# Attention denominators of a three-stage transformer block: two split fp32r products instead of one plain fp32 product

## The chip, the cores and the metric

The kernel runs on one core of one Trainium2 chip. Its time is the device time of one execution in microseconds (us). The engines are named as in the profile: PE (TensorE matmul; PEld is its weight load), DVE (VectorE), ACT (ScalarE), POOL (GpSimd) and SP (SyncE, which here only issues transfers).

## The reference, cut to what matters

The block has three parts: cross attention, a causal linear attention with 16 heads of 64, and a mixture of 8 experts. The change lies in the second part:

```python
q = jax.nn.elu(q) + 1.0
k = jax.nn.elu(k) + 1.0
k_cum = jnp.cumsum(k, axis=1)
kv = jnp.cumsum(k[..., None, :] * v[..., :, None], axis=1)
numerator = jnp.einsum('bthj,bthij->bthi', q, kv)
denominator = jnp.einsum('bthj,bthj->bth', q, k_cum)
out = numerator / (denominator[..., None] + 1e-06)
```

The kernel computes this by masked scores: per batch entry and head it forms k times q (32 x 32), multiplies it by the causal mask (the tile `att`), and the denominator is the sum of `att` over the keys.

## The kernel before, in words

There are 64 batch entries of 32 tokens. Four entries make a tile of 128 rows, and there are 16 tiles. The cross attention goes tile by tile and lasts to about 130 us. The linear attention goes in 8 steps r of two tiles each, from about 132 us to 423 us, with a drain after the last; the experts fill the rest.

In the linear attention the large products are made of fp32 values split in two fp32r halves: `mm3` issues hi times hi, hi times lo and lo times hi (lines L437 to L439). Small products and the denominators are plain fp32.

Every engine runs its own program, written out in order, and the engines meet by semaphores only. In step r the order on each engine is this.

- PE (`astep` under `block.tensor`): eight blocks of q and k columns (`a_qks`, blocks 0 to 7, 12 matmuls each), with the denominators of step r-1 (`a_dens`, L611) between block 1 and block 2; then four blocks of gate columns (`a_gates`); then `a_nums` of step r-1 (L623) and `a_values`, once for each of the two tiles; the transposes for step r+1; then `a_proj` of step r-1 and `a_scores` (L602), again per tile. Block n of q and k from 4 on may start only when DVE has finished block n-4 of the same step (it takes over the PSUM bank), and gate block n only when DVE has finished block n+4. `a_nums` needs the normalised `att`.
- ACT: for every block Relu and Exp (L870, L873), with the copies of the denominators (`den_ev`, L897) between block 1 and block 2; then four Tanh for the gates, the high halves of the gated output (`gated_hi`, L892) and the copies of the values. From step 2 on a step ends in a Sqrt (L916) for the next layer norm, and then the next Exp has to load its function table first (ACT_TABLE_LOAD). So steps 3 to 7 begin with such a load, and steps 1 and 2 don't.
- DVE: `masks` (L1152) makes `att` of step r-1 out of the scores; `elu` (L1161) finishes each of the blocks 0 to 7 after its Exp; between them stand the four reciprocals of the denominators (`recip`, L1169) and the two multiplications by them (`norm_att`, L1174); then the layer norm rows, `gated` (L1181), `gated_lo` (L1191) and more.
- SP loads the weights of the experts (L348), 2 MB for each, into places that the attention's tiles leave free one after the other. Expert 1 is loaded right after the cross attention's last inputs, the other seven from the end of the linear attention on. The experts' first step waits for all eight.

Of the kernel before, what the change touches and what calls it, by code (L numbers as in the profile page):

```python
# [16 lines left out]
P = 128  # L17
# [57 lines left out]
def wait(eng, sem, value):  # L75

    if isinstance(value, int) and value <= 0:
        return
    eng.wait_ge(sem, value)
# [24 lines left out]
def build(nc, ctx, a, out):  # L104
# [10 lines left out]
    def place(name, shape, dtype=F32, where="low"):  # L115
        n = 4
        for d in shape[1:]:
            n *= d
        t = nc.alloc_sbuf_tensor_at(name, shape, dtype, offset=at[where])
        at[where] += (n + 31) // 32 * 32  # L120
        return t
# [67 lines left out]
    den = place("den", [P, 2, FC * 2 * T], where="late")  # L189
    neg = place("neg", [P, 2, 512], where="late")  # L190
    ex = place("ex", [P, 2, 512], where="late")
    w_out_lo = place("w_out_lo", [P, FC, D], F32R, "late")
    goh = place("goh", [P, FC, 2 * P], F32R, "late")
    assert at["late"] <= TOP_ADDR - 2 * DC * 4 * HF * 4
# [72 lines left out]
    def sem(name):  # L267
# [24 lines left out]

    (g_part, g_var, g_sq, g_rs, g_ln, g_tr, g_xT, g_mm, g_sc, g_max, g_idx, g_keep) = (sem("g_" + n) for n in (
        "part", "var", "sq", "rs", "ln", "tr", "xT", "mm", "sc", "max", "idx", "keep"))
    r_step, r_d, r_e1, r_both, r_rank, r_what, r_in, r_tab, r_map, r_done = (
        sem("r_" + n) for n in ("step", "d", "e1", "both", "rank", "what", "in", "tab", "map", "done"))
    o_init = sem("o_init")
# [13 lines left out]
    def _(sp):  # L311
# [35 lines left out]
        def load_expert(e):  # L347
            sp.dma_start(w13[:, e, :, :, :].rearrange("p w c h -> p (w c h)"), a["w13"][e, :, :]).then_inc(l_w13, 16)  # L348

        load_expert(1)  # L350
        sp.wait_ge(a_v, 4 * NT // 2)
        for e in range(E // 2, E):
            load_expert(e)
        sp.wait_ge(a_num, NT)
        sp.wait_ge(a_y, NT // 2)
        for e in (2, 3):
            load_expert(e)
# [76 lines left out]
    def _(pe):  # L434
# [171 lines left out]
                m.then_inc(a_sc, 1)  # L606

        def a_dens(r):
            wait(pe, a_att, 2 * r + 2)
            for s in range(2):  # L610
                pe.matmul(ps[:, 4 + s, :], con[:, C_TWOS:C_TWOS + P], att[:, s, :, :, :].rearrange("p c h t -> p (c h t)"),  # L611
                          start=True, stop=True).then_inc(a_den, 1)

        def a_nums(r, s):
            wait(pe, a_norm, 2 * r + s + 1)
# [23 lines left out]
        def astep(r, u):  # L639
            before = valid(r - 1, NR)  # L640
            wait(pe, a_lo, r + 1)
            a_qks(r, range(0, 2))
            if before:
                a_dens(r - 1)
            a_qks(r, range(2, 8))
            a_gates(r)
            for s in range(2):
                if before:
                    a_nums(r - 1, s)
                a_values(r, s)  # L650
            a_trs(r + 1)
            for s in range(2):
                if before:
                    a_proj(r - 1, 1 - u, s)
                a_scores(r, s)
# [133 lines left out]
    def _(act):  # L789
# [96 lines left out]
        def gated_hi(r, u, s):  # L886
# [3 lines left out]
            for k in range(2):  # L890
                cs = slice(4 * k, 4 * k + 4)
                act.activation(goh[:, cs, rows], goT[:, u, cs, rows], ACT.Copy).then_inc(a_gh, 1)  # L892

        def den_ev(r):
            for s in range(2):
                wait(act, a_den, 2 * r + s + 1)
                act.activation(den[:, s, :], ps[:, 4 + s, :], ACT.Identity, bias=con[:, C_EPS2:C_EPS2 + 1]).then_inc(a_de, 1)  # L897
# [24 lines left out]

        def astep(r, u):
            before = valid(r - 1, NR)
            elu_parts(r, range(0, 2))
            if before:
                den_ev(r - 1)
            elu_parts(r, range(2, 8))
            gates(r, u)
            for s in range(2):  # L930
                if before:
                    gated_hi(r - 1, 1 - u, s)
                values(r, s)
            a_hi_ev(r + 1)
            if r == 0:
                w_out_round()
            g_sqrt(r - 2)

        def drain(r, u):
            for k in range(3):  # L940
                g_xT_ev(k)
            den_ev(r)
            for k in range(3, 6):
                g_xT_ev(k)
            g_sqrt(r - 1)
            gated_hi(r, u, 0)
            g_xT_ev(6)
            gated_hi(r, u, 1)
            g_sqrt(r)
            g_xT_ev(7)  # L950

        a_hi_ev(0)
        for r in range(NR):
            astep(r, r % 2)
# [80 lines left out]
    def _(dve):  # L1035
# [112 lines left out]
        def masks(r):  # L1148
            mask = con[:, C_MASK:C_MASK + T].rearrange("p (a b t) -> p a b t", a=1, b=1).to_broadcast([P, 2, FC, T])
            wait(dve, a_sc, r + 1)  # L1150
            for h in range(2):
                dve.tensor_tensor(att[:, :, :, h, :], ps[:, 4 + h, :].rearrange("p (s c t) -> p s c t", s=2, c=FC), mask,  # L1152
                                  ALU.mult).then_inc(a_att, 1)

        def elu(r, n):
            if not valid(r, NR):
                return
            wait(dve, a_e, 8 * r + n + 1)
            wait(dve, a_sc, r)
            dst = kT if n % 2 else qT  # L1160
            dve.scalar_tensor_tensor(dst[:, n // 2 * 2:n // 2 * 2 + 2, :].rearrange("p c n -> p (c n)"), ps[:, n % 4, :], 0.0,  # L1161
                                     ex[:, n % 2, :], ALU.max, ALU.add).then_inc(a_qku, 1)
# [71 lines left out]
        def astep(r, u):  # L1234
            before = valid(r - 1, NR)
            if before:
                masks(r - 1)
            elu(r, 0)
            elu(r, 1)
            recip(r - 1, 0)  # L1240
            elu(r, 2)
            recip(r - 1, 1)
            if before:
                norm_att(r - 1, 0)
            elu(r, 3)
            elu(r, 4)
            recip(r - 1, 2)
            elu(r, 5)
            elu(r, 6)
            recip(r - 1, 3)  # L1250
            elu(r, 7)
# [68 lines left out]

        def drain(r, u):
            masks(r)
            g_stats(r - 1)
            recip(r, 0)
            recip(r, 1)
# [194 lines left out]
```

## Time and profile before

| | |
|---|---|
| median of 3 runs | 890.28 us (888.61 to 892.51) |
| the profiled execution | 885.24 us, its span 883.4 us |
| mean granted PE clock | 0.947 of 2.4 GHz |
| PE busy | 798.3 us (90%) |
| DVE busy | 640.1 us (72%) |
| ACT busy | 553.5 us (63%) |

Busy times are sums over the span. They say how much an engine works, and not when it is waited for. Start times in the rows further down count from the start of the span. The length of a merged row reaches from the start of its first instruction to the end of its last, and PE's instructions overlap, so the spacing of starts is what a matmul costs.

### The profile page before, as it was taken

How to read it: one execution, taken by the hardware profiler on the slowest of the kernel's cores; microseconds unless marked ns; L12 is line 12 of the kernel's file. 1: busy time of each engine (PE TensorE's matmuls, PEld its weight loads, DVE VectorE, ACT ScalarE, POOL GpSimd, SP SyncE). 2: the span in 40 equal slices, each digit the busy share in tenths (PEclk: the TensorE clock that was granted, in tenths of full speed). 3: DMA queues.
4: the chain of work that ended last, by engine and by line, in shares of the span. 5: the costliest groups of instructions: out<-in, count | busy, mean ns of one | idle time of the engine just before them, and what ended most of it. 6: DMA issues, size and time to landing. Idle time of an engine off the chain costs nothing.

```text
span 883.4 us, 24070 instructions
## 1 busy us (share of the span) xinstructions
PE 798.3 (90%) x9166; PEld 693.4 (78%) x9166; DVE 640.1 (72%) x1026; ACT 553.5 (63%) x855; POOL 247.2 (28%) x149
## 2 busy tenths in 40 slices
PE   3899869899999999999673599999999999999994
PEld 2555539899899998988663488888888888888883
DVE  3234342557576675755667599999999999999992
ACT  2433326736466465654211499899899899999981
POOL 1343420000000000000000145455455455465551
PEclk9899998999999999999765699999999999999997
DMA  9799950000000000003734245455445445455442
GB/s 350 288 391 397 376 234 1 3 3 13 27 3 26 15 14 27 3 26 116 305 137 173 65 135 147 129 137 151 127 132 153 130 137 149 129 137 149 130 127 52
DMA packets 31766, 115.86 MB, mean 131 GB/s; under 512 B 4465, under 2 KB 11570, under 8 KB 26578
## 3 DMA queue, kind: packets, MB, share of 16 engines
q1 hardware_dynamic: 22834, 100.17, 32.2%
q0 software_dynamic: 8864, 14.69, 7.9%
q8 instruction: 54, 0.88, 0.4%
q14 instruction: 14, 0.11, 0.0%
HBM read 105.27 MB, written 9.57 MB: 130 GB/s over the span
## 4 chain that ended last, share of the span: by engine, by line
PE 82%; DMA 8%; DVE 5%; issue 2%; SPq 1%; ACT 1%; POOLq 0%; DVEq 0%; ACTq 0%
PE ps L437 22%; PE ps L439 21%; PE ps L438 21%; DMA ctx_t<-in_ctxT 6%; PE ps L770 4%; PE ps L623 2%; PE ps L602 2%; PE ps L611 2%; PE ps L494 1%; PE ps L516 1%; PE ps L733 1%; PE ps L673 1%; PE ps L722 1%; DVE bn L1041 1%; PE ps L513 1%
## 5 line engine op out<-in xcount | busy, mean ns | idle before, releaser
L1367 DVE TENSOR_TENSOR w_lo<-w,w_hi 128x1024 fp32r<-128x1024 f32 x156 | 187.1, 1222 | 1.4 <-issue 1.4
L966 ACT ACTIVATE w_hi<-w 128x1024 fp32r x156 | 161.3, 1061 | 9.8 <-DMA w<-in_w 9.5
L423 POOL DMA_INDIRECT out_x<-y_sb,slot_row x39 | 124.7, 3197 | 117.9 <-ACT y_sb L998 117.9
L437 PE MATMUL ps<-w_hi,xh 128*128 128x512 f32 x312 | 126.4, 405 | 1.4 <-DVE xl L1453 1.3
L439 PE MATMUL ps<-w_hi,xl 128*128 128x512 f32 x312 | 122.6, 393 | 0.0
L438 PE MATMUL ps<-w_lo,xh 128*128 128x512 f32 x312 | 122.3, 392 | 0.0
L437 PE MATMUL ps<-xT_hi,wa_hi 128*128 128x256 f32 x384 | 113.2, 295 | 1.5 <-DVE xT_lo L1145 1.5
L438 PE MATMUL ps<-xT_lo,wa_hi 128*128 128x256 f32 x384 | 109.3, 285 | 0.0
L439 PE MATMUL ps<-xT_hi,wa_lo 128*128 128x256 f32 x384 | 109.3, 285 | 0.0
L977 ACT ACTIVATE w_hi<-w_sb 128x1024 fp32r<-128x1024 f32 x78 | 82.7, 1061 | 29.3 <-DMA w_sb<-in_w 18.8
L412 POOL DMA_INDIRECT xs_sb<-xn_d,slot_row x39 | 67.9, 1740 | 104.3 <-PE ps L733 76.4
L437 PE MATMUL ps<-w_hi,hh 128*128 128x256 f32 x312 | 92.0, 295 | 2.9 <-DVE hl L1460 2.9
L1439 DVE TENSOR_TENSOR w_lo<-w_sb,w_hi 128x1024 fp32r<-128x1024 f32 x78 | 92.1, 1222 | 2.1 <-ACT w_hi L977 2.1
L439 PE MATMUL ps<-w_hi,hl 128*128 128x256 f32 x312 | 88.8, 285 | 0.0
L438 PE MATMUL ps<-w_lo,hh 128*128 128x256 f32 x312 | 88.7, 284 | 0.0
L437 PEld LDWEIGHTS ps<-xT_hi,wa_hi 128*128 128x128 f32 x384 | 74.1, 193 | 3.7 <-issue 3.4
L438 PEld LDWEIGHTS ps<-xT_lo,wa_hi 128*128 128x128 f32 x384 | 74.1, 193 | 1.7 <-issue 1.7
L439 PEld LDWEIGHTS ps<-xT_hi,wa_lo 128*128 128x128 f32 x384 | 75.0, 195 | 0.0
L870 ACT ACTIVATE neg<-ps 128x512 f32<-128x512 f32 x64 | 38.1, 596 | 57.6 <-PE ps L439 56.2
L437 PEld LDWEIGHTS ps<-w_hi,xh 128*128 128x128 f32 x312 | 58.9, 189 | 13.3 <-DVE xl L1453 1.9
L439 PEld LDWEIGHTS ps<-w_hi,xl 128*128 128x128 f32 x312 | 59.0, 189 | 13.0
L438 PEld LDWEIGHTS ps<-w_lo,xh 128*128 128x128 f32 x312 | 59.1, 189 | 11.3
(201 smaller groups left out, 1703.3 us busy)
## 6 DMA issues: line engine op xcount, KB each, us to landing
w_sb<-in_w SPq DMA_DIRECT2D x78, 512.0 KB
ctx_t<-in_ctxT SPq DMA_DIRECT2D x16, 1028.0 KB, 7.2
ctx_n<-in_ctxN SPq DMA_DIRECT2D x16, 1024.0 KB
w<-in_w SPq DMA_DIRECT2D x8, 2048.0 KB, 12.2
stage<-in_w_a SPq DMA_DIRECT2D x16, 256.0 KB, 5.3
x_all<-in_x SPq DMA_DIRECT2D x4, 512.0 KB, 6.6
out_x<-x_all POOLq DMA_DIRECT2D x8, 256.0 KB, 3.2
xn_d<-xn POOLq DMA_DIRECT2D x8, 256.0 KB, 3.0
```

What stands on the lines that cost most here:

```text
L412: pool.indirect_dma_start(xs_sb[:, :], None, xn_d, bass.IndirectOffsetOnAxis(slot_row[:, t:t + 1], 0)).then_inc(f_xs, 16)
L423: pool.indirect_dma_start(out, bass.IndirectOffsetOnAxis(slot_row[:, t:t + 1], 0), y_sb[:, :], None, compute_op=ALU.add).then_inc(f_st, 16)
L437: pe.matmul(dst, l_hi, r_hi, start=first, stop=False)
L438: pe.matmul(dst, l_hi, r_lo, start=False, stop=False)
L439: return pe.matmul(dst, l_lo, r_hi, start=False, stop=last)
L602: m = pe.matmul(ps[b * T:(b + 1) * T, 4 + h, (s * FC + c) * T:(s * FC + c + 1) * T], kT[rows, c, tok], qT[rows, c, tok], start=True, stop= ...
L770: m = pe.transpose(ps[:, 4 + c // 4, (c % 4) * P:(c % 4 + 1) * P], h_sb[:, c * P:(c + 1) * P], ident)
L870: act.activation(neg[:, n % 2, :], ps[:, n % 4, :], ACT.Relu, scale=-1.0).then_inc(a_neg, 1)
L966: act.activation(w_hi[:, c, :].rearrange("p (c n) -> p c n", c=DC), w13[:, bass.ds(e, 1), c % 2, :, c // 2 * 512:(c // 2 + 1) * 512].rearr ...
L977: act.activation(w_hi[:, 4 + c, :], src, ACT.Copy).then_inc(f_dhi, 1)
L1367: dve.tensor_tensor(w_lo[:, c, :].rearrange("p (c n) -> p c n", c=DC), w13[:, bass.ds(e, 1), c % 2, :, c // 2 * 512:(c // 2 + 1) * 512].re ...
L1439: dve.tensor_tensor(w_lo[:, 4 + c, :], src, w_hi[:, 4 + c, :].bitcast(F32), ALU.subtract).then_inc(f_dlo, 1)
```

## The change

It has four parts. The denominators are now two fp32r products that add up in PSUM, of a matrix `twos` (a copy of the same constants as fp32r) with `att_hi` and with `att_lo`. ACT makes `att_hi` (`att_high`, two copies of 128x512 per step, at the head of its step), and DVE makes `att_lo` as `att` minus `att_hi` (`att_low`, two subtractions of 128x512 per step, right after `masks`). The denominators stand after block 3 on PE, and no more after block 1; the copies `den_ev` follow on ACT after block 3 as well, and on DVE the first reciprocal comes after `elu` of block 3. The new tiles lie in the place of expert 1's weights, so that expert's load is moved to where the last `a_nums` is done.

```diff
+    att_hi = nc.alloc_sbuf_tensor_at("att_hi", [P, 2, FC * 2 * T], F32R, offset=W13_AT + EXP_BYTES)
+    att_lo = nc.alloc_sbuf_tensor_at("att_lo", [P, 2, FC * 2 * T], F32R, offset=W13_AT + EXP_BYTES + 8 * FC * 2 * T)
+    twos = nc.alloc_sbuf_tensor_at("twos", [P, P], F32R, offset=W13_AT + EXP_BYTES + 16 * FC * 2 * T)
...
-        load_expert(1)
         sp.wait_ge(a_v, 4 * NT // 2)
         for e in range(E // 2, E):
             load_expert(e)
         sp.wait_ge(a_num, NT)
+        load_expert(1)
         sp.wait_ge(a_y, NT // 2)
...
         def a_dens(r):
+            pe.wait_ge(a_two, 1)
             wait(pe, a_att, 2 * r + 2)
             for s in range(2):
-                pe.matmul(ps[:, 4 + s, :], con[:, C_TWOS:C_TWOS + P], att[:, s, :, :, :].rearrange("p c h t -> p (c h t)"),
-                          start=True, stop=True).then_inc(a_den, 1)
+                wait(pe, a_al, 2 * r + s + 1)
+                pe.matmul(ps[:, 4 + s, :], twos[:, :], att_hi[:, s, :], start=True, stop=False)
+                pe.matmul(ps[:, 4 + s, :], twos[:, :], att_lo[:, s, :], start=False, stop=True).then_inc(a_den, 1)
...
             a_qks(r, range(0, 2))
+            a_qks(r, range(2, 4))
             if before:
                 a_dens(r - 1)
-            a_qks(r, range(2, 8))
+            a_qks(r, range(4, 8))
...
+        def att_high(r):
+            wait(act, a_att, 2 * r + 2)
+            wait(act, a_den, 2 * r)
+            for s in range(2):
+                act.activation(att_hi[:, s, :], att[:, s, :, :, :].rearrange("p c h t -> p (c h t)"), ACT.Copy).then_inc(a_ah, 1)
...
-            elu_parts(r, range(0, 2))
+            if before:
+                att_high(r - 1)
+            elu_parts(r, range(0, 4))
             if before:
                 den_ev(r - 1)
-            elu_parts(r, range(2, 8))
+            elu_parts(r, range(4, 8))
...
             for k in range(3):
                 g_xT_ev(k)
+            att_high(r)
             den_ev(r)
...
+        act.activation(twos[:, :], con[:, C_TWOS:C_TWOS + P], ACT.Copy).then_inc(a_two, 1)
...
+        def att_low(r):
+            wait(dve, a_den, 2 * r)
+            for s in range(2):
+                wait(dve, a_ah, 2 * r + s + 1)
+                dve.tensor_tensor(att_lo[:, s, :], att[:, s, :, :, :].rearrange("p c h t -> p (c h t)"), att_hi[:, s, :].bitcast(F32),
+                                  ALU.subtract).then_inc(a_al, 1)
...
             if before:
                 masks(r - 1)
+            if before:
+                att_low(r - 1)
             elu(r, 0)
             elu(r, 1)
+            elu(r, 2)
+            elu(r, 3)
             recip(r - 1, 0)
-            elu(r, 2)
+            elu(r, 4)
             recip(r - 1, 1)
             if before:
                 norm_att(r - 1, 0)
-            elu(r, 3)
-            elu(r, 4)
+            elu(r, 5)
             recip(r - 1, 2)
-            elu(r, 5)
             elu(r, 6)
             recip(r - 1, 3)
             elu(r, 7)
```

On ACT the order at the head of step 3 before the change, from the first Relu (`neg`) over the copies of the denominators (`den`) to the Exp (`ex`) of block 2, is this:

```order
L870 ACTIVATE neg<-ps 128x512
L873 ACT_TABLE_LOAD
L873 ACTIVATE ex<-neg 128x512
L870 ACTIVATE neg<-ps 128x512
L873 ACTIVATE ex<-neg 128x512
L897 ACTIVATE den<-ps,con 128x512 x2
L870 ACTIVATE neg<-ps 128x512
L873 ACTIVATE ex<-neg 128x512
```

With the change the same place has the two copies into `att_hi` ahead of the first Relu, and `den` behind the Exp of block 3:

```order
L905 ACTIVATE att_hi<-att 128x512 x2
L877 ACTIVATE neg<-ps 128x512
L880 ACT_TABLE_LOAD
L880 ACTIVATE ex<-neg 128x512
L877 ACTIVATE neg<-ps 128x512
L880 ACTIVATE ex<-neg 128x512
L877 ACTIVATE neg<-ps 128x512
L880 ACTIVATE ex<-neg 128x512
L877 ACTIVATE neg<-ps 128x512
L880 ACTIVATE ex<-neg 128x512
L910 ACTIVATE den<-ps,con 128x512 x2
L877 ACTIVATE neg<-ps 128x512
```

What moved: two copies came in ahead of everything, and two more blocks stand ahead of the denominators' copies. The table load stays between the Relu and the Exp of block 0.

On DVE the same step before the change, from `masks` (`att<-ps,con`) to the reciprocal after block 4 and the blocks behind it (`elu` writes `qT` for even blocks and `kT` for odd ones), is this:

```order
L1152 TENSOR_TENSOR att<-ps,con 128x16x32 x2
L1161 SCALAR_TENSOR_TENSOR qT<-ps,ex 128x512
L1161 SCALAR_TENSOR_TENSOR kT<-ps,ex 128x512
L1169 RECIPROCAL den<-den 128x256
L1161 SCALAR_TENSOR_TENSOR qT<-ps,ex 128x512
L1169 RECIPROCAL den<-den 128x256
L1174 TENSOR_TENSOR att<-att,den 128x512
L1161 SCALAR_TENSOR_TENSOR kT<-ps,ex 128x512
L1161 SCALAR_TENSOR_TENSOR qT<-ps,ex 128x512
L1169 RECIPROCAL den<-den 128x256
L1161 SCALAR_TENSOR_TENSOR kT<-ps,ex 128x512
L1161 SCALAR_TENSOR_TENSOR qT<-ps,ex 128x512
```

With the change:

```order
L1169 TENSOR_TENSOR att<-ps,con 128x16x32 x2
L1176 TENSOR_TENSOR att_lo<-att,att_hi 128x512 x2
L1185 SCALAR_TENSOR_TENSOR qT<-ps,ex 128x512
L1185 SCALAR_TENSOR_TENSOR kT<-ps,ex 128x512
L1185 SCALAR_TENSOR_TENSOR qT<-ps,ex 128x512
L1185 SCALAR_TENSOR_TENSOR kT<-ps,ex 128x512
L1193 RECIPROCAL den<-den 128x256
L1185 SCALAR_TENSOR_TENSOR qT<-ps,ex 128x512
L1193 RECIPROCAL den<-den 128x256
L1198 TENSOR_TENSOR att<-att,den 128x512
L1185 SCALAR_TENSOR_TENSOR kT<-ps,ex 128x512
L1193 RECIPROCAL den<-den 128x256
```

What moved: two subtractions into `att_lo` came in after `masks`, and the first reciprocal stands after four blocks of `elu`, where two stood before it. The last reciprocal still stands ahead of the `elu` of block 7.

## Rows read from the trace of the kernel before

**Rows 1.** Windows: length, busy of PE, PEld, DVE, ACT, POOL, clock, DMA, GB/s.

```profile
160.80:164.20 3.40, 2.35 (x47) 2.29 (x48) 1.95 (x4) 1.68 (x4) 0.00 (x0) 0.67 0.03 7
230.00:320.00 90.00, 90.00 (x1841) 82.95 (x1840) 57.53 (x107) 50.25 (x83) 4.30 (x6) 1.00 0.06 20
440.00:450.00 10.00, 9.31 (x125) 8.85 (x115) 7.06 (x52) 1.82 (x4) 0.00 (x0) 0.50 0.01 2
```

**Rows 2.** Timeline of DVE, step 5: start, length, line, operation, count.

```profile
309.82 1.29 DVE L1152 TENSOR_TENSOR att<-ps,con 128x512 f32<-128x512 f32 x2 [0.53 <-PE ps L602]
...
315.75 1.74 DVE L1169 RECIPROCAL den<-den 128x256 f32<-128x256 f32 x1
317.45 0.69 DVE L1161 SCALAR_TENSOR_TENSOR qT<-ps,ex 128x512 f32<-128x512 f32 x1
...
326.11 0.63 DVE L1161 SCALAR_TENSOR_TENSOR kT<-ps,ex 128x512 f32<-128x512 f32 x1
```

**Rows 3.** Timeline of PE, step 5.

```profile
309.71 0.38 PE L437 MATMUL ps<-xT_hi,wa_hi 128*128 128x256 f32 x1
...
312.64 1.88 PE L611 MATMUL ps<-att,con 128*128 128x512 f32 x4
...
314.47 0.28 PE L438 MATMUL ps<-xT_lo,wa_hi 128*128 128x256 f32 x1
...
328.58 1.49 PE L623 MATMUL ps<-att,v_sb 32*64 32x32 f32 x128
...
330.34 0.39 PE L438 MATMUL ps<-wa_lo,xT_hi 128*128 128x512 f32 x1
330.57 0.39 PE L439 MATMUL ps<-wa_hi,xT_lo 128*128 128x512 f32 x1
...
346.11 0.38 PE L437 MATMUL ps<-xT_hi,wa_hi 128*128 128x256 f32 x1
```

**Rows 4.** Timeline of ACT, step 5, with what ended its idle time.

```profile
311.42 0.60 ACT L870 ACTIVATE neg<-ps 128x512 f32<-128x512 f32 x1 [6.81 <-PE ps L439]
312.04 1.28 ACT L873 ACT_TABLE_LOAD   x1
313.33 0.63 ACT L873 ACTIVATE ex<-neg 128x512 f32<-128x512 f32 x1
...
315.02 1.25 ACT L897 ACTIVATE den<-ps,con 128x512 f32<-128x512 f32 x2
...
318.01 0.63 ACT L873 ACTIVATE ex<-neg 128x512 f32<-128x512 f32 x1
...
331.55 1.16 ACT L892 ACTIVATE goh<-goT 128x512 fp32r<-128x512 f32 x2 [2.27 <-DVE goT L1181]
```

**Rows 5.** Timeline of DVE, step 2.

```profile
200.74 1.29 DVE L1152 TENSOR_TENSOR att<-ps,con 128x512 f32<-128x512 f32 x2 [1.07 <-PE ps L602]
...
216.72 0.63 DVE L1161 SCALAR_TENSOR_TENSOR kT<-ps,ex 128x512 f32<-128x512 f32 x1
```

**Rows 6.** Timeline, all engines, the drain after the last step.

```profile
426.05 1.88 PE L611 MATMUL ps<-att,con 128*128 128x512 f32 x4
426.25 0.60 ACT L921 ACTIVATE xT<-ps 128x512 f32<-128x512 f32 x1 [0.87 <-PE ps L663]
...
432.36 0.29 ACT L916 ACTIVATE rstd<-rstd,eps 128x2 f32<-128x2 f32 x1
```

**Rows 7.** Timeline of PE at the last transfer of ctx_t.

```profile
116.97 0.86 PE L494 MATMUL ps<-ctx_t,qkT 128*32 128x257 f32 x12 [1.41 <-DMA ctx_t<-in_ctxT]
```

**Rows 8.** First conversion of expert weights: durations, first and last start.

```profile
L966 ACT ACTIVATE w_hi<-w x156: 1042/1058/1088, 478.4 to 853.5; 128x1024 fp32r x156
```

**Rows 9.** The chain that ended last, between attention and experts.

```profile
480.09 7.07 PE ps L722 x32
```

**Rows 10.** The chain that ended last, at the end of step 0.

```profile
159.60 2.24 issue
```

More of the change, by code:

```diff
@@ L294, in build @@
         "part", "var", "sq", "rs", "ln", "tr", "xT", "mm", "sc", "max", "idx", "keep"))
+    a_ah, a_al, a_two = (sem(n) for n in ("a_att_hi", "a_att_lo", "a_two"))
     r_step, r_d, r_e1, r_both, r_rank, r_what, r_in, r_tab, r_map, r_done = (
@@ L1322, in drain @@
             masks(r)
+            att_low(r)
             g_stats(r - 1)
```

## The prediction

> **What bounds the kernel now.** I read the windows first, then the timeline of one step of the linear attention engine by engine, then the chain of work that ended last around it. In the windows [rows 1] the reader is to see that PE is busy for 90.00 of the 90 us from 230 to 320, at the full granted clock, while DVE and ACT have work for 57.53 and 50.25 of them. So inside the steps PE sets the time, and whatever PE issues less is a gain, provided that nobody makes it wait. A share of 64% for DVE seems to promise that. It is an average over the step, though, and the change touches the one stretch of the step in which DVE is full.
>
> That stretch is seen in DVE's timeline of step 5 [rows 2]. The first reciprocal starts at 315.75 and the `elu` of block 7 at 326.11, and in these 10.36 us lie four reciprocals of 1.70 (315.75 to 317.45), five `elu` of 0.60 and one multiplication, that is 6.8 + 3.0 + 0.6, with nothing left over. PE's last gate block may start only when that `elu` is done, at 326.74. PE's own pace is in [rows 3]: from the end of the denominators, 314.35, to `a_nums` at 328.58 it does ten blocks, 1.42 us each, so it starts the last gate block at about 327.1. The slack between the two is 0.3 us. Before the change this order just fits.
>
> **The change part by part, in step 5.** The denominators on PE: L611 starts at 312.64 and the second matmul behind it at 314.47 [rows 3]; less the 0.12 of the matmul between, the two plain fp32 products cost 1.71 us. The new ones are four fp32r matmuls of 128x512, and that shape follows itself after 0.23 us (330.34 to 330.57) [rows 3], so 0.92 us. PE is to gain 0.79 us in each of seven steps.
>
> ACT: `masks` ends at 309.82 + 1.29 = 311.11 [rows 2]. The nearest row for a copy to fp32r out of SBUF is `goh`, two of 128x512 in 1.16 us, the next instruction starting 0.1 before their end [rows 4]. So the two new copies hold ACT from 311.17 to 312.23, and the first Relu, at 311.42 before, starts at 312.23. From that Relu to the Exp of block 3 it took 318.01 - 311.42 = 6.59 us, of which the two copies `den` (1.25, less the overlap 1.14) now come later: 5.45 us are left, table load of 1.28 included [rows 4]. So the Exp of block 3 runs from 317.68 to 318.31. PE has finished block 3 at 309.7 + 4 x 1.42 = 315.4 and doesn't hold this up. The `elu` of block 3 follows at 318.35, and the first reciprocal at 318.95; the first `den` copy, from 318.22 to 318.91, is just there. That is 3.20 us later than the 315.75 of before.
>
> DVE: the two `att_low`, 1.3 us as `masks` is [rows 2], lie in a gap of DVE, between 311.8 and 313.1, for the first `elu` comes after 314. PE reads them at 315.4, so they and the wait for `twos` (one copy at the start, while ACT idles) cost nothing; without this cover att_low would cost its 1.3. What counts is behind the first reciprocal. Two `elu` fewer stand there, so 10.36 - 1.2 = 9.2 us: the `elu` of block 7 starts at 328.15 and ends at 328.8, 2.0 us later than before.
>
> PE: gate blocks 1 to 3 now wait for the `elu` of blocks 5 to 7. The last starts at 328.85, and `a_nums` at 330.4 in place of 328.58. So the step gets longer by 1.8 us, where without a wait it would be shorter by 0.79. Queued behind the waiting gate block on PE are `a_nums`, the values and the projections, and DVE's `gated` and ACT's copies follow these at the old distances; so nothing is regained up to the next step's start (346.11 before) [rows 3].
>
> Steps 3 to 7 begin with the table load, as step 5: 5 x 1.8 = 9.0 us. In steps 1 and 2 there is none. In step 2 `masks` ends at 202.03 [rows 5]; two copies to 203.14, then 5.45 - 1.28 = 4.17 to the Exp of block 3 at 207.31, the reciprocal at 208.6, and the `elu` of block 7 at 217.8 against 216.72. Less the slack of 0.3 to 0.5 that is 0.6 to 0.8 us; I take 0.6, twice 1.2 us.
>
> The table load lies inside the chain that now decides. It takes 1.28 us: the Relu ends at 312.02, the load runs from 312.04, the Exp starts at 313.33 [rows 4]. The Trainium skill (ScalarE: Activation LUTs, What ACT_TABLE_LOAD costs) has 1283 ns for the load and about 1380 ns of drain on top, 2.66 us for every switch. By that page each of the five steps would be another 1.4 us late and the sum 6.9 us higher; the trace has no room for the drain, and the sum goes by the trace.
>
> The drain: the denominators run to 426.05 + 1.88 = 427.93 [rows 6]. Now ACT makes `att_hi` after its copy that ends at 426.85, until 427.9; the second `att_low` ends at 428.7 and the last product at 429.2. PE's transposes behind it are 1.2 us late, and with them the Sqrt at 432.36, for which DVE's third reciprocal waits: +1.2 us. If the late order hides nothing but its own gain it is -0.8, if a low clock follows on PE's wait it is +3.
>
> Expert 1's load: before, it ran behind the last inputs of the cross attention. PE waited 1.41 us for the last `ctx_t` [rows 7], so at most 1.4 us could come back. The transfer of `ctx_t` was issued before the load, and I take nothing; 1.4 is the other end. At its new place, about 441, DMA is idle (share 0.01 from 440 to 450) [rows 1]. SP's queue behind it waits for `a_y` anyway. The first conversion of expert weights is at 478.4 [rows 8], when the chain still runs through the routing on PE, at 480.09 for 7.07 us [rows 9], so even a later load would have cover.
>
> Sum: 9.0 + 1.2 + 1.2 = 11.4 us on the profiled execution's 885.24, which makes 896.6. That execution lies 5.0 us below the median of the runs shown; on the median, 890.28, it is 901.7 us.
>
> **The rivals.** *The vector work is hidden and PE's saving stays* (0.08): 8 x 0.79 = 6.3 us less, 884.0. The 64% of DVE speaks for it. It takes a first reciprocal at 316.35 or earlier in step 5, 2.6 us ahead of my 318.95; against it stand the queues, where the Exp of block 3 comes ahead of it.
>
> *The wait is there but small* (0.14): if ACT's and DVE's blocks run 1.2 to 2.4 us closer together than the rows of before let me think, the step changes by +0.6 to -0.6 us, and the time stays within 4.4 us of 890.
>
> *The clock falls as well* (0.18). After an idle time of 2.24 us at 159.60 [rows 10] the clock granted from 160.8 to 164.2 was 0.67, so part of it at 1.2 GHz [rows 1]. The new waits are three of about 0.9 us with a block between each. If PE ran the gate blocks at 1.2 GHz, only the last would count, since DVE sets the start of each: 1.4 us more in five steps, 7 us, 909.
>
> *My forecast* (0.60): its own range is 897 to 907, from 0.4 us of error per step (2.8), the ends of the drain (-2.0, +1.8) and the spread of the runs (2).
>
> **How the numbers follow.** A difference below 0.5%, 4.4 us, can hardly be told from none in this kernel. Slower by more than that are the forecast and the clock, 0.60 + 0.18 and a little of the small wait, 0.79; faster by more is the hidden case, 0.08; 0.13 stay for the same. The range of 8 in 10 goes from 893 (the small wait's upper end) to 910.
>
> **What would show it.** In the profile after, PE's denominators should be four matmuls 0.23 apart. The steps with the table load should last 38.2 us in place of 346.11 - 309.71 = 36.4. PE should wait in the gate blocks for `qT` and `kT` of DVE, about 2.6 us in a step, and DVE should have no idle time between the first reciprocal and the last `elu`. The first reciprocal should start 9.2 us after a step's first matmul, not 6.0. I am wrong if steps get shorter than 36.4 us: then the first reciprocal started earlier than I think, or the waits of PE are for something else.

## The result

The changed kernel is slower: 905.03 us median of 8 runs (898.57 to 912.91), against 889.44 us for the kernel before (8 runs, 886.04 to 894.43). One of the new runs, the 912.91, was in a slower state of the chip and stays out of the ratio. The ratio is 1.0128 with a 95% interval of 1.0091 to 1.0164, that is 11.4 us with 8.1 to 14.6. The plain medians lie further apart, 15.6 us, and the means of the eight runs before and the other seven runs after 13.4 us; the record doesn't say how the ratio weighs its runs. So the kernel is slower for certain, and by how much is known only as some 8 to 16 us. The forecast was 11.4 us more, 901.7 us on a median of 890.28.

Of the page of the changed kernel these are the span, the busy line and the chain that ended last, by engine.

```profile
span 903.1 us, 24124 instructions
...
PE 803.4 (89%) x9166; PEld 700.2 (78%) x9166; DVE 653.0 (72%) x1042; ACT 558.0 (62%) x872; POOL 242.5 (27%) x149
...
PE 65%; DVE 14%; DMA 9%; issue 5%; ACT 4%; SPq 1%; POOLq 0%; DVEq 0%; ACTq 0%
```

Before, the chain was PE for 82% of the span and DVE for 5%. Now DVE has 14% and ACT 4% of it, though DVE's busy time grew by 12.9 us only (640.1 to 653.0). The new profiled execution is 19.7 us longer in its span than the one of before, which is more than the ratio says. Of these, 4.0 us lie ahead of the linear attention, where the two programs differ in expert 1's load alone (it starts at 136.54 instead of 132.57, and in the other twelve executions anywhere from 134.3 to 145.0, whatever the kernel); 8.3 lie in its steps 1 to 7 and 5.3 in the drain, as measured below; and about 2 lie in the experts.

The windows of the changed kernel, as in [rows 1]: length, busy time of PE, PEld, DVE, ACT and POOL, granted clock, DMA share, GB/s. The first answers to the one of 230 to 320 there; the other four are the drain.

```profile
230.00:320.00 90.00, 86.48 (x1843) 80.18 (x1834) 58.30 (x111) 46.98 (x80) 4.29 (x6) 1.00 0.06 20
434.00:438.00 4.00, 3.49 (x124) 2.97 (x108) 1.29 (x2) 1.31 (x3) 0.00 (x0) 1.00 1.02 424
438.00:442.00 4.00, 2.17 (x7) 1.81 (x7) 2.88 (x11) 2.18 (x5) 0.00 (x0) 0.63 1.02 431
442.00:446.00 4.00, 4.00 (x21) 4.00 (x22) 3.84 (x3) 1.20 (x2) 0.00 (x0) 0.50 1.02 430
446.00:450.00 4.00, 4.00 (x22) 4.00 (x20) 0.00 (x0) 1.32 (x3) 0.00 (x0) 0.50 0.45 193
```

PE now has 86.48 us of work in 90 where it had 90.00, at the same full clock. In the drain it is at 1.2 GHz from some point between 438 and 442 on, and it stays there although it is busy for 4.00 of 4.00 us.

PE's timeline of step 5 answers to [rows 3]; the first matmul of the step starts at 318.05.

```profile
318.05 0.38 PE L441 MATMUL ps<-xT_hi,wa_hi 128*128 128x256 f32 x1
...
323.80 0.39 PE L617 MATMUL ps<-att_hi,twos 128*128 128x512 f32 x1
324.04 0.40 PE L618 MATMUL ps<-att_lo,twos 128*128 128x512 f32 x1
...
332.58 0.39 PE L441 MATMUL ps<-xT_hi,wa_hi 128*128 128x256 f32 x1 [0.63 <-DVE kT L1185]
...
334.79 0.39 PE L441 MATMUL ps<-xT_hi,wa_hi 128*128 128x256 f32 x1 [0.56 <-DVE qT L1185]
...
336.99 0.39 PE L441 MATMUL ps<-xT_hi,wa_hi 128*128 128x256 f32 x1 [0.55 <-DVE kT L1185]
...
338.57 1.49 PE L629 MATMUL ps<-att,v_sb 32*64 32x32 f32 x128
```

The reader is to see three things. The split products follow each other after 0.24 us. The gate blocks 1, 2 and 3 (332.58, 334.79, 336.99) each wait for an `elu` of DVE. And `a_nums` starts 20.52 us after the step's first matmul, where it was 18.87. The three waits are 1.74 us of idle time, but they cost more than that: the blocks now start 2.2 us apart, where PE's pace before was 1.42.

ACT in the same step, as in [rows 4]: the two copies into `att_hi`, the first Relu, the table load, the Exp of block 3, the copies `den`.

```profile
319.48 1.16 ACT L905 ACTIVATE att_hi<-att 128x512 fp32r<-128x512 f32 x2 [6.54 <-DVE att L1169]
320.54 0.58 ACT L877 ACTIVATE neg<-ps 128x512 f32<-128x512 f32 x1
321.14 1.28 ACT L880 ACT_TABLE_LOAD   x1
...
325.88 0.63 ACT L880 ACTIVATE ex<-neg 128x512 f32<-128x512 f32 x1
326.42 1.25 ACT L910 ACTIVATE den<-ps,con 128x512 f32<-128x512 f32 x2
```

DVE in the same step, as in [rows 2]: `masks`, `att_low`, the first reciprocal, the `elu` of block 7.

```profile
318.16 1.29 DVE L1169 TENSOR_TENSOR att<-ps,con 128x512 f32<-128x512 f32 x2 [0.53 <-PE ps L606]
320.22 1.29 DVE L1176 TENSOR_TENSOR att_lo<-att,att_hi 128x512 fp32r<-128x512 f32 x2 [0.77 <-ACT att_hi L905]
...
327.15 1.74 DVE L1193 RECIPROCAL den<-den 128x256 f32<-128x256 f32 x1
...
336.31 0.63 DVE L1185 SCALAR_TENSOR_TENSOR kT<-ps,ex 128x512 f32<-128x512 f32 x1
```

The first reciprocal starts 9.10 us after the step's first matmul (6.04 before), and the last `elu` 18.26 us after it (16.40 before). The step takes 38.02 us (318.05 to 356.07), where it took 36.40.

The drain of the changed kernel, as in [rows 6]: ACT's copies, PE's first split product and the Sqrt behind which the last reciprocals wait.

```profile
438.27 1.14 ACT L905 ACTIVATE att_hi<-att 128x512 fp32r<-128x512 f32 x2
...
439.83 0.77 PE L617 MATMUL ps<-att_hi,twos 128*128 128x512 f32 x1 [2.09 <-DVE att_lo L1176]
...
449.77 0.29 ACT L929 ACTIVATE rstd<-rstd,eps 128x2 f32<-128x2 f32 x1
```

PE waits 2.09 us for `att_low` there. From the end of step 7 (434.85) to the Sqrt it is 14.92 us; before it was 9.59 (422.77 to 432.36).

### The profile page after: what moved, and what is told of

The parts are those of the page before. It is cut to its first block, busy times and chain, and to the rows that moved or that the text cites. A ratio compares the mean times of both kernels' runs of the same rounds, so it can differ in the third digit from the quotient of the medians.

```text
span 903.1 us, 24124 instructions
## 1 busy us (share of the span) xinstructions
PE 803.4 (89%) x9166; PEld 700.2 (78%) x9166; DVE 653.0 (72%) x1042; ACT 558.0 (62%) x872; POOL 242.5 (27%) x149
## 4 chain that ended last, share of the span: by engine, by line
PE 65%; DVE 14%; DMA 9%; issue 5%; ACT 4%; SPq 1%; POOLq 0%; DVEq 0%; ACTq 0%
PE ps L441 17%; PE ps L443 16%; PE ps L442 16%; DMA ctx_t<-in_ctxT 6%; DVE den L1193 6%; PE ps L777 3%; PE ps L629 2%; PE ps L606 2%; DVE kT L1185 2%; ACT ex L880 1%; PE ps L498 1%; ACT neg L877 1%; PE ps L520 1%; DVE qT L1185 1%; PE ps L680 1%
## 5 line engine op out<-in xcount | busy, mean ns | idle before, releaser
L427 POOL DMA_INDIRECT out_x<-y_sb,slot_row x39 | 119.7, 3069 | 123.7 <-ACT y_sb L1015 123.7
L441 PEld LDWEIGHTS ps<-w_hi,xh 128*128 128x128 f32 x312 | 58.9, 189 | 13.4 <-DVE xl L1480 1.9
L410 POOL DMA_DIRECT2D xn_d<-xn x8 | 5.7, 708 | 222.8 <-DVE xn L1255 222.8
## 6 DMA issues: line engine op xcount, KB each, us to landing
w<-in_w SPq DMA_DIRECT2D x8, 2048.0 KB, 11.4
```

The lines of the kernel that those rows point to most:

```text
L427: pool.indirect_dma_start(out, bass.IndirectOffsetOnAxis(slot_row[:, t:t + 1], 0), y_sb[:, :], None, compute_op=ALU.add).then_inc(f_st, 16)
L441: pe.matmul(dst, l_hi, r_hi, start=first, stop=False)
```

## The experiments

The places are measured in the same way in every kernel: a step runs from its first matmul to that of the next step, and the drain from its first transpose to the first Sqrt in it. Steps 1, 6 and 7 hold stretches in which PE waits for nothing that the profile shows, in all kernels, and are left out of the table. Single steps of the table hold such a stretch too: step 3 of `e_before_table` (0.90 us), step 3 of `e_load1` (0.46), and step 4 of `e_best` and of `e_recip_late` (0.46 and 0.40). Ratios are those of the timed runs to the kernel before on the same chip. Two of the kernels are the originals, profiled a second time.

| kernel | steps 3, 4, 5 (us) | drain to the Sqrt (us) | ratio |
|---|---|---|---|
| before | 36.44, 36.38, 36.40 | 9.59 | 1 |
| changed | 38.02, 38.03, 38.02 | 14.92 | 1.0128 (1.0091 to 1.0164) |
| e_order_only | 37.59, 37.64, 37.63 | 11.90 | 1.0117 (1.0084 to 1.0151) |
| e_split_only | 36.98, 36.96, 36.97 | 14.93 | 1.0070 (1.0038 to 1.0101) |
| e_table | 37.23, 36.91, 36.91 | 15.20 | 1.0108 (1.0068 to 1.0148) |
| e_drain | 38.07, 38.03, 38.02 | 15.11 | 1.0120 (1.0033 to 1.0206) |
| e_drain_plain | 38.02, 38.02, 38.01 | 12.37 | 1.0111 (1.0065 to 1.0156) |
| e_best | 35.66, 36.16, 35.35 | 10.47 | 0.9929 (0.9891 to 0.9967) |
| e_best2 | 35.92, 35.93, 35.92 | 10.19 | 0.9944 (0.9917 to 0.9970) |
| e_load1 | 36.98, 36.38, 36.37 | 15.92 | 1.0000 (0.9969 to 1.0032) |
| e_recip_late | 35.76, 36.16, 35.59 | 14.92 | 1.0003 (0.9975 to 1.0031) |
| e_before_table | 37.66, 36.50, 36.50 | 9.77 | one execution |
| e_before_again | 36.30, 36.38, 36.29 | 11.68 | one execution |
| e_after_again | 38.06, 38.06, 38.02 | 14.70 | one execution |

### The order alone

```diff
--- before
-            a_qks(r, range(0, 2))
+            a_qks(r, range(0, 4))
             if before:
                 a_dens(r - 1)
-            a_qks(r, range(2, 8))
+            a_qks(r, range(4, 8))
```

The same was done to `elu_parts` and `den_ev` on ACT and to the reciprocals on DVE.

> The kernel before with one part of the change: the plain fp32 denominators, their copies on ScalarE and the reciprocals on VectorE stand behind block 3 and in the order of the change; no split, no new copies, expert 1's load at its old place. My theory (the chain from the first Relu over the Exp of block 3, the first reciprocal and the four reciprocals to the elu of block 7 holds up the gate blocks): a step with a table load takes 0.8 us more than the 36.4 before, 37.2, because the first reciprocal starts 2.4 us later and two elu fewer stand behind it. That makes about 5 us over the steps, ratio 1.006. Rival (the new copies and subtractions on ScalarE and VectorE make the loss, the order is harmless): steps of 36.4 us and ratio 1.000.

DVE in step 5, which starts at 322.04: the first reciprocal, the `elu` of block 4, the `elu` of block 7.

```profile
330.38 1.74 DVE L1169 RECIPROCAL den<-den 128x256 f32<-128x256 f32 x1
332.42 0.69 DVE L1161 SCALAR_TENSOR_TENSOR qT<-ps,ex 128x512 f32<-128x512 f32 x1 [0.29 <-ACT ex L873]
...
339.88 0.63 DVE L1161 SCALAR_TENSOR_TENSOR kT<-ps,ex 128x512 f32<-128x512 f32 x1
```

The steps are 1.2 us longer, with nothing split: the order alone makes most of the loss in a step, and the rival falls. It is more than the 0.8 I expected, and the ratio, 1.0117, is well above the expected 1.006; 2.3 us of that are its drain (11.90 against 9.59). The first reciprocal starts 8.34 us after the step's start, as reckoned (8.4), but the last `elu` comes 9.50 us behind it and not 9.2, since the `elu` of block 4 waits 0.29 us for its Exp. (That this comes from the plain products, which still take 1.7 us of PE ahead of block 4, is argued only.)

### The split alone

```diff
--- after
             a_qks(r, range(0, 2))
-            a_qks(r, range(2, 4))
             if before:
                 a_dens(r - 1)
-            a_qks(r, range(4, 8))
+            a_qks(r, range(2, 8))
```

ACT and DVE get their old order back too.

> The changed kernel with the denominators, their copies and the reciprocals back at the old places, behind block 1; the split stays, with its two copies ahead of the first Relu and its two subtractions behind masks. My theory: the copies move the first Relu and all behind it by 0.8 us, the order has 0.3 us of slack, so the step takes 0.5 us more than before, 36.9, and PE waits a further 0.5 us for att_lo ahead of the denominators, in the place of the wait at the gates. Ratio 1.004 without the drain, 1.009 with a drain as long as in the changed kernel. Rival (the order makes the loss, the split itself pays its 0.79 us): steps of 35.6 us, ratio 0.995 to 1.000.

PE in step 5, which starts at 310.19: the first split product, and the matmul of block 7.

```profile
313.19 0.47 PE L617 MATMUL ps<-att_hi,twos 128*128 128x512 f32 x1
...
322.43 0.39 PE L441 MATMUL ps<-xT_hi,wa_hi 128*128 128x256 f32 x1 [1.17 <-DVE kT L1184]
```

DVE: the first reciprocal and the last `elu`.

```profile
316.99 1.74 DVE L1192 RECIPROCAL den<-den 128x256 f32<-128x256 f32 x1
...
327.34 0.63 DVE L1184 SCALAR_TENSOR_TENSOR kT<-ps,ex 128x512 f32<-128x512 f32 x1
```

The step takes 36.97 us, 0.6 more than before, as the theory has it (36.9). The 0.79 us that the split saves on PE show nowhere. They are lost at block 7 of q and k, which waits 1.17 us for the `elu` of block 3: the two copies ahead of the first Relu put that whole row of `elu` back, and the first reciprocal starts 6.80 us after the step's start instead of 6.04. The wait of 0.5 us ahead of the denominators did not come about; the first split product starts 3.00 us after the step's start, as the plain one did (2.93). All this holds for the steps with a table load. Step 2, which has none, takes 35.73 us, 0.6 less than before (36.29), and the seven steps together take 260.2 us, as long as before (260.4). So in this kernel the steps break even, and its ratio of 1.0070 is about its longer drain (14.93 against 9.59 us).

### The table load taken out of the chain

```diff
--- after
             act.activation(rstd3[:, :], rstd3[:, :], ACT.Sqrt, bias=eps[:, 0:1]).then_inc(g_sq, 1)
+            if early_table:
+                act.activation(warm[:, :], eps[:, 0:1], ACT.Exp)
...
-            g_sqrt(r - 2)
+            g_sqrt(r - 2, r < NR - 1)
```

> The changed kernel with one addition: after the Sqrt at the end of each step a one-column Exp, so that the function table for the next step is loaded while ScalarE is idle. My theory: the load's 1.28 us leave the chain to the last elu, steps 3 to 7 fall from 38.0 to 36.8 us, the length of step 2, which has no load; 6 us less in all, ratio to the kernel before 1.006. Rival (VectorE's own amount of work, the subtractions included, sets the step): its work is unchanged and the step stays at 38.0 us, ratio 1.013.

ACT in step 5: the first Relu and, right behind it, the first Exp.

```profile
321.70 0.58 ACT L878 ACTIVATE neg<-ps 128x512 f32<-128x512 f32 x1
322.31 0.63 ACT L881 ACTIVATE ex<-neg 128x512 f32<-128x512 f32 x1
```

Steps 4 and 5 fall to 36.91 us (36.8 expected; step 3 takes 37.23) with DVE's work unchanged. So it is not the amount of work on DVE that sets the step, but how late its run of reciprocals and `elu` begins, and the 1.28 us of the load were part of that. In the timed runs little of it is seen: the ratio was to be 1.006 and is 1.0108 (1.0068 to 1.0148), which can't be told from the changed kernel's. In the profiled execution the seven steps take 263.2 us, 5.5 less than in the changed kernel, so the step's part rests on the profile alone. The load was there before the change too, and cost nothing then, as the next run shows.

```diff
--- before
             act.activation(rstd3[:, :], rstd3[:, :], ACT.Sqrt, bias=eps[:, 0:1]).then_inc(g_sq, 1)
+            if early_table:
+                act.activation(warm[:, :], eps[:, 0:1], ACT.Exp)
...
-            g_sqrt(r - 2)
+            g_sqrt(r - 2, r < NR - 1)
```

> The kernel before with the one-column Exp after each Sqrt alone, so that the table load leaves the head of steps 3 to 7. Theory: before the change PE's own pace sets the step, and the last elu has 0.3 us of slack, so the steps stay at 36.4 us though the first Exp comes 1.3 us earlier. Rival (the vector chain sets the step before as well): steps of 35.1 to 36.0 us. The drain is the plain one: 10 to 12 us by theory A, anything by theory B.

DVE in step 5, which starts at 313.01: the first reciprocal and the last `elu`.

```profile
318.05 1.74 DVE L1172 RECIPROCAL den<-den 128x256 f32<-128x256 f32 x1
...
329.24 0.63 DVE L1164 SCALAR_TENSOR_TENSOR kT<-ps,ex 128x512 f32<-128x512 f32 x1
```

The first reciprocal starts 5.04 us after the step's start, a whole microsecond earlier than before, and the step is not shorter (36.50), in this one execution. In the kernel before PE sets the step; the chain of Exp and reciprocals does so only once it is late by more than its slack.

### Expert 1's load

```diff
--- before
-        load_expert(1)
         sp.wait_ge(a_v, 4 * NT // 2)
...
         sp.wait_ge(a_num, NT)
+        load_expert(1)
```

> The kernel before with one part of the change: expert 1's load stands after the last a_nums, where the change has it. My theory: nothing changes, as the load ran behind the last inputs before and is covered by the routing now; ratio 1.000 (0.997 to 1.003), the linear attention starts 0 to 1.4 us earlier. Rival (the moved load delays the experts' first step, or the cross attention's end moves by the 4 us seen between the two profiled executions): ratio 1.003 or more.

The ratio is 1.0000 (0.9969 to 1.0032), so the moved load costs and brings nothing that can be measured, within 3 us either way. In the changed kernel the conversions of expert weights begin at 496.1, 1.5 us ahead of the routing's long matmul at 497.60, about as far ahead as before (1.7 us) [rows 8, 9].

```profile
L983 ACT ACTIVATE w_hi<-w x156: 1040/1063/1087, 496.1 to 871.3; 128x1024 fp32r x156
```

Its drain is another matter, and comes below.

### The drain

I held the wait of 2.09 us for what lengthens the drain.

```diff
--- after
-            for k in range(3):
+            for k in range(2):
                 g_xT_ev(k)
             att_high(r)
+            g_xT_ev(2)
             den_ev(r)
```

> The changed kernel with the two copies into att_hi in the drain one place earlier on ScalarE, ahead of its third copy of the router's inputs. In the changed kernel PE waits 2.1 us there, and the drain up to the Sqrt takes 14.9 us in place of 9.5. My theory: the wait costs about 1.5 us itself and makes the granted clock fall to 1.2 GHz, which costs the rest; with the wait at 0.7 us or less the clock holds and the drain up to the Sqrt takes 10 us, ratio 1.007 to 1.008. Rival (the later reciprocals of the drain make it longer, the clock would have fallen anyway): the drain gets shorter by 1 us only, to 14 us, ratio 1.012. The steps stay at 38.0 us by both.

PE's third split product in the drain, and two windows of it.

```profile
439.17 0.80 PE L617 MATMUL ps<-att_hi,twos 128*128 128x512 f32 x1 [0.52 <-issue]
...
432.00:436.00 4.00, 3.90 (x117) 3.60 (x118) 1.29 (x2) 1.42 (x3) 0.00 (x0) 0.62 1.00 425
...
440.00:444.00 4.00, 4.00 (x21) 3.91 (x21) 3.46 (x3) 1.29 (x2) 0.00 (x0) 0.50 0.99 422
```

The longest wait is 0.52 us, and the drain still takes 15.11 us, at 1.2 GHz. But the clock fell early in this execution, in the window from 432 to 436, and the first split product starts at 437.45: it was low before the place where the wait would have been. So the run shows that a drain with split products can be long without the wait, and it does not show that the wait is harmless where the clock is still full when it comes. I took my theory for refuted, and the next expectation says so; it was not. The ratio, 1.0120 (1.0033 to 1.0206), is too wide to tell the expected 1.007 from the rival's 1.012.

```diff
--- after
             g_trs(2)
-            a_dens(r)
+            a_dens_plain(r)
```

Here `a_dens_plain` is the old `a_dens`, and `att_high` and `att_low` are gone from the drain alone.

> The changed kernel with the drain's denominators (those of step 7) as in the kernel before: plain fp32, no split in the drain. The drain with a shorter wait still took 15 us at 1.2 GHz, so the wait of 2.1 us is not what lengthens it. My theory now: the plain products, 1.7 us of gapless PE work at 2.4 GHz and twice as long at 1.2, are part of what keeps or brings back the higher clock in the drain; the split products are half of that. With them the drain up to the Sqrt takes 9.6 us (as before) to 11.9 us (as with the order alone), 3 to 5 us less than 14.9; ratio 1.008 to 1.010. Rival (the clock falls in the drain because the steps end later against the expert weights' transfers, or by chance): it stays at about 15 us. The steps stay at 38.0 us by both.

PE's plain products in the drain, and the window behind them.

```profile
438.83 3.57 PE L615 MATMUL ps<-att,con 128*128 128x512 f32 x4
...
443.00:447.00 4.00, 4.00 (x34) 4.00 (x33) 2.56 (x3) 1.59 (x4) 0.00 (x0) 0.83 0.97 414
```

The drain takes 12.37 us, just above the range I gave. The clock was low from its start, comes back with the last of the products, and falls again ahead of the Sqrt (0.83 in that window). The ratio, 1.0111, can't be told from the changed kernel's. But then the drain of the run that only moves the load took 15.92 us, with plain products in it. Two windows of that run:

```profile
429.00:433.00 4.00, 4.00 (x9) 1.93 (x7) 1.14 (x1) 1.44 (x3) 0.00 (x0) 0.50 1.00 428
...
437.00:441.00 4.00, 4.00 (x22) 4.00 (x20) 0.00 (x0) 1.38 (x3) 0.00 (x0) 0.50 0.10 37
```

It was at 1.2 GHz from 425 to 441. So the clock can stay low in the old drain as well, and I profiled more drains.

> The kernel before, unchanged, for a second profiled execution. Theory A: its drain takes 9.6 to 12 us up to the Sqrt; theory B: anything from 10 to 16. The steps take 36.4 us; the start of the linear attention lies anywhere from 132 to 142 us.

> The changed kernel, unchanged, for a second profiled execution. Theory A: its drain takes 15 us up to the Sqrt; theory B: anything from 10 to 16. The steps take 38.0 us.

These two gave 11.68 and 14.70 us, and `e_before_table` gave 9.77. The last one is a kernel that the next section needs anyway: the mended order with the split left in the drain.

> The changed kernel with VectorE's order mended as in the fastest version so far, but with the split denominators left in the drain. Theory A (the split products in the drain leave PE too little gapless work there, and the clock stays at 1.2 GHz): the drain up to the Sqrt takes 15 us, as in the four profiled executions with a split drain, against 10 to 12 in five of six with plain products there; ratio 0.996 to 0.998 against 0.993 with the plain ones. Theory B (the clock in the drain falls by chance in either kernel, as it did once with the plain products): the drain takes anything from 10 to 16 us, ratio 0.993 as with the plain ones. The steps take 35.6 us by both.

Two windows of its drain.

```profile
423.00:427.00 4.00, 2.67 (x9) 2.31 (x9) 3.38 (x11) 2.18 (x4) 0.00 (x0) 0.59 1.00 424
427.00:431.00 4.00, 4.00 (x21) 4.00 (x21) 3.34 (x3) 0.70 (x2) 0.00 (x0) 0.50 1.02 430
```

Its drain takes 14.92 us. Together: with split products in the drain all six executions took 14.70 to 15.20 us, mean 15.0 ((14.92 + 14.93 + 15.20 + 15.11 + 14.92 + 14.70) / 6). With plain ones seven of eight took 9.59 to 12.37 us and one 15.92, mean 11.5 ((9.59 + 11.90 + 12.37 + 10.47 + 10.19 + 15.92 + 9.77 + 11.68) / 8). So the split in the drain goes with a longer drain, by 3.5 us in the mean, and theory B leaves no reason for six out of six.

What it is in the split that does it stays open, for the split brings two things into the drain, shorter gapless work of PE (theory A) and the wait for `att_low`. Windows of three drains: the changed kernel, the kernel before, and `e_best`.

```profile
438.00:439.00 1.00, 0.00 (x0) 0.00 (x0) 0.01 (x1) 1.00 (x3) 0.00 (x0) 1.00 0.91 377
439.00:440.00 1.00, 0.17 (x1) 0.20 (x2) 1.00 (x2) 0.41 (x1) 0.00 (x0) 0.51 1.17 496
...
421.00:425.00 4.00, 3.42 (x112) 3.12 (x112) 2.08 (x6) 0.82 (x2) 0.00 (x0) 0.57 1.00 426
424.80:428.00 3.20, 3.20 (x19) 2.24 (x19) 0.91 (x8) 1.89 (x4) 0.00 (x0) 1.00 1.04 437
...
424.00:428.00 4.00, 2.68 (x17) 1.80 (x16) 2.73 (x2) 1.66 (x3) 0.00 (x0) 1.00 1.03 438
```

In the changed kernel the clock is full until 439 and low from there, in the middle of the wait (437.74 to 439.83). The other four split drains that reach the wait at the full clock, with the same 2.09 us of it, fall in the wait as well or, in one case, 0.3 us behind it, 4.3 to 5.2 us after the drain's start; the sixth is `e_drain`. The plain drains have no such wait, and none falls at that place. Three of them (`e_best`, `e_best2`, `e_before_table`) are at the full clock up to the Sqrt. The other five are low at the drain's start: the kernel before is back at the full clock at 424.8, ahead of its plain products (426.05) [rows 6], three are back towards the end of these products (`e_order_only`, `e_drain_plain`, `e_before_again`), and `e_load1` never. So the wait, my first theory, is a rival as strong as theory A: it fits five of the six, and theory A has `e_drain` on its side. No run has the split products at the full clock without the wait, or the wait without them.

### The mended order

```diff
--- after
             recip(r - 1, 0)
             elu(r, 4)
-            recip(r - 1, 1)
-            if before:
-                norm_att(r - 1, 0)
             elu(r, 5)
-            recip(r - 1, 2)
+            recip(r - 1, 1)
             elu(r, 6)
-            recip(r - 1, 3)
             elu(r, 7)
+            if before:
+                norm_att(r - 1, 0)
+            recip(r - 1, 2)
+            recip(r - 1, 3)
```

This is `e_recip_late`; `e_best` has the plain products in the drain in addition.

> The changed kernel with VectorE's order mended and the plain denominators in the drain: the reciprocals 2 and 3 stand behind the elu of block 7, and reciprocal 1 behind the elu of block 5, and the first multiplication behind the elu of block 7. My theory: only the elu are waited for by the gate blocks, and a_nums of the first tile needs reciprocals 0 and 1 alone, so PE waits no more, and the split pays its 0.79 us: steps of 35.6 us, 5.5 us less than before over seven steps; ratio 0.994 to 0.997. Rival (VectorE and ScalarE as a whole are too late, whatever their order): steps above 36.4 us, ratio over 1.000.

DVE in step 5 of `e_best`: the first reciprocal and the `elu` of block 7; then PE: the step's first matmul and `a_nums`.

```profile
320.55 1.74 DVE L1198 RECIPROCAL den<-den 128x256 f32<-128x256 f32 x1
...
326.21 0.68 DVE L1190 SCALAR_TENSOR_TENSOR kT<-ps,ex 128x512 f32<-128x512 f32 x1
...
311.44 0.39 PE L441 MATMUL ps<-xT_hi,wa_hi 128*128 128x256 f32 x1
...
329.30 1.49 PE L635 MATMUL ps<-att,v_sb 32*64 32x32 f32 x128
```

The first reciprocal is as late as in the changed kernel, 9.11 us after the start. The last `elu` comes 14.77 us after it and not 18.26, and `a_nums` starts at 17.86, 1.0 us earlier than in the kernel before. Steps 3 and 5 take 35.66 and 35.35 us, 0.8 and 1.05 less than before: now the split's 0.79 us are there, and in step 5 a little more, which isn't explained. (Step 4 takes 36.16 us, only 0.2 less; PE is busy for 35.70 of them, and the profile names nothing for the other 0.46.) The ratio is 0.9929 (0.9891 to 0.9967), so this version beats both. With the split in the drain it is 1.0003 (0.9975 to 1.0031), above the 0.996 to 0.998 of theory A, though the interval reaches in, and clear of theory B's 0.993. The two were timed on different chips, each against its own runs of the kernel before; the profiled drains differ by 4.5 us of the 6.6 between the ratios.

> The split with the denominators, their copies and the reciprocals at the old places, the early table load of the one-column Exp, and the plain denominators in the drain. Theory: steps 3 to 7 come down from 37.0 us to the 35.7 us that step 2 had with the split at the old place, where there is no table load; ratio 0.994 to 0.998. Rival (PE's wait for att_lo ahead of the denominators remains, with or without the load): 36.4 us and more, ratio 1.000.

This is the split alone with the early table load and the plain drain; its edits are shown above. Its steps take 35.92 us, between the 35.7 of the theory and the 36.4 of the rival and nearer to the first, and its ratio is 0.9944 (0.9917 to 0.9970). So the old order works as well, once the load is out of the way of the two copies.

## Why the prediction was right, point by point

**PE's saving.** Right: four split products 0.23 to 0.24 us apart, and `e_best` collects 0.8 and 1.05 us in two of three steps.

**ACT's start.** Right: the first Relu starts 2.49 us after the step's first matmul, 2.52 forecast (312.23 less 309.71), and the Exp of block 3 7.83 us after it, 7.97 forecast.

**The first reciprocal and the last elu.** Right: 9.10 and 18.26 us, forecast 9.24 and 18.44. There is no idle time of DVE between them. PE's waits were to be 2.6 us in a step; they are 1.74 us of idle time, and 2.4 by what they cost, which is the 1.62 us of the longer step and the 0.79 saved. That the wait follows from the order was shown by moving the reciprocals behind the last `elu`, and that ACT's copies and the load are part of the chain by `e_split_only` and `e_table`.

**The price of a step.** 1.62 us in steps 3 to 5 instead of 1.8, and 0.47 in step 2 (36.76 against 36.29) instead of 0.6. The seven steps together are 268.7 us against 260.4, so 8.3 us longer, where I had 10.2. In steps 3 to 5 the order by itself costs 1.2 us a step (`e_order_only`) and the split with its copies 0.6 (`e_split_only`); together they make 1.62.

**The drain.** This is the term of the sum that was mis-sized: "+1.2 us", with +3 as its upper end for a low clock. Between the two profiled executions it is 5.3 us, and 3.5 us in the mean over fourteen. The 1.2 us were for PE's wait, and that is the smaller part: the router's products behind the denominators now start 6.8 us after the drain's start (441.68 less 434.85), where they started at 5.0 (427.76 less 422.77). That is 1.8 us, part of it already the split products' own low clock, and the other 3.5 are the router's transposes and products at 1.2 GHz. The low clock had been put down as the upper end only, for a clock that follows on PE's wait; in the changed kernel it does fall during that wait, but that the wait is the cause is not shown. The two errors, 1.9 us too much in the steps and 2.3 too little in the drain, cancel. So that the forecast's 11.4 is also the ratio's 11.4 is luck, and by the medians, 15.6 us, it would have been 4 us off. The range of 893 to 910 holds by either.

**Expert 1's load.** Right as far as can be told: nothing beyond the 0.3% of the interval, by a run of its own.

**The rivals.** The hidden vector work would have needed the first reciprocal 2.6 us earlier; it came 0.14 earlier. The small wait would have left the step within 0.6 us of 36.4; it changed by 1.6. The clock did not fall in the steps: it is 1.00 from 230 to 320, with three waits in each step. It fell in the drain instead. The table load was as the trace of before has it, and not as the Trainium skill has it (ScalarE: Activation LUTs, What ACT_TABLE_LOAD costs): with the load off the chain step 5 falls from 38.02 to 36.91 us, by 1.1 and not by the 2.66 that the page gives for a switch.

## What to carry to other kernels

An engine that is busy for two thirds of a step can still be full in one stretch of it. Add up its instructions between the first and the last that another engine waits for, and compare the sum with the time that the other engine gives it, before anything is put in front of that stretch. A saving on the engine that sets the time is worth nothing if the same change makes its supplier later than the slack, here 0.3 us; and within the supplier's order, what is waited for soonest should come first, long reciprocals behind it. And a split that pays in a full step can cost time elsewhere: in the drain, where PE has little other work, it came with a low clock in six of six executions, and the mended order is faster with the plain products there (0.9929 against 1.0003).

## What was not expected of the hardware

In the drain PE's granted clock stayed at 1.2 GHz while PE was busy for all of two windows of 4 us (442 to 450 in the changed kernel), with transposes and products of 8 columns; the split products lie just ahead, also at the low clock. Of the eight drains with plain fp32 products three never lost the full clock before the Sqrt, four lost it around their start and got it back, and one did not. Why some get it back isn't shown: PE is busy for 4.00 of 4.00 us at the low clock in drains of either kind. In the middle of the steps three waits of about 0.6 us in 5 us, which I had given 0.18 for a fall of the clock, did not lower it in any of five steps.
